# Two seams between experts, one more early tile, and layer 1's first rows turned bank by bank

## The reference

```python
def sage_conv(x, src, dst, Wl, b, Wr):          # twice per layer, relu between
    mean = segment_sum(x[src], dst) / max(count(dst), 1)
    return mean @ Wl.T + b + x @ Wr.T
x = x + gnn0(layernorm(x))
x = x + ffn0(layernorm(x))     # 8 experts, 256 -> 512 -> 256, each row takes the 2 with the best scores
x = x + gnn1(layernorm(x))
x = x + ffn1(layernorm(x))     # a shared MLP and 4 small experts, weighted top 2
# ffn0, one expert: gelu(x @ W1[e] + b1[e]) @ W2[e] + b2[e], summed over the row's two experts
```

## Time and profile before

| | us |
|---|---|
| median of 3 runs | 1255.82 (1254.37 to 1258.06) |
| profiled execution | 1258.41 |
| its span | 1256.9 |
| TensorE busy | 1170.8 (93%) |
| VectorE busy | 582.1 (46%) |
| ScalarE busy | 356.5 (28%) |
| GpSimd busy | 161.4 (13%) |

### The profile page before, as it was taken

The page is one execution under the profiler, slowest core; times in us unless marked ns, Lnnn a source line. Parts: engine busy times, 40 slices in busy tenths (PEclk is TensorE's granted clock), DMA queues, the critical chain, the costliest instruction groups (busy, mean ns, idle before and its releaser), DMA issues. The chain is left out here.

```text
span 1256.9 us, 22265 instructions
## 1 busy us (share of the span) xinstructions
PE 1170.8 (93%) x7928; PEld 884.9 (70%) x7928; DVE 582.1 (46%) x1656; ACT 356.5 (28%) x767; POOL 161.4 (13%) x152
## 2 busy tenths in 40 slices
PE   5979999998999996998999959999999999999998
PEld 3658888885667884777888746655556678876675
DVE  7978888844445768111111155100024455346644
ACT  3554444432220002322333233300012201033433
POOL 4100000000000436443344400000000000000000
PEclk9979999999999997999999969999989999998999
DMA  6500000025653336355654342110046535226101
GB/s 203 167 25 13 22 18 13 21 60 142 179 141 98 111 115 189 65 106 103 137 110 87 68 116 85 59 53 30 30 122 176 152 95 173 81 73 192 42 21 39
DMA packets 134352, 117.30 MB, mean 93 GB/s; under 512 B 23302, under 2 KB 122697, under 8 KB 134272
## 3 DMA queue, kind: packets, MB, share of 16 engines
q1 hardware_dynamic: 102640, 76.36, 21.3%
q0 software_dynamic: 12368, 18.62, 7.6%
q10 hardware_dynamic: 19264, 21.24, 4.9%
HBM read 67.01 MB, written 48.76 MB: 92 GB/s over the span
## 5 line engine op out<-in xcount | busy, mean ns | idle before, releaser
L1334 PE MATMUL b_pa<-adj,l_parts 128*128 (+2 forms) x1078 | 144.0, 285 | 3.7 <-ACT ring L1267 3.7
L1334 PEld LDWEIGHTS b_pa<-adj,l_parts 128*128 128x128 f16 x1078 | 101.0, 98 | 26.9 <-issue 5.5
L1273 ACT ACTIVATE adj<-b_pw 128x450 f32 (+1 forms) x176 | 86.6, 546 | 97.4 <-PE b_pw L1318 92.4
L2512 PE MATMUL l_sum<-l_parts,ring 128*128 128x256 f32 x448 | 104.0, 385 | 5.0 <-ACT ring L2582 2.3
L2647 POOL DMA_INDIRECT x<-ring,l_ids_now x56 | 87.5, 1562 | 132.8 <-DVE ring L2612 92.7
L601 DVE TENSOR_TENSOR ring<-it,key 128x900 f16<-128x900 f16 (+1 forms) x176 | 88.8, 547 | 30.8 <-PE b_pw L1318 30.7
L2512 PEld LDWEIGHTS l_sum<-l_parts,ring 128*128 128x128 f32 x448 | 82.9, 190 | 22.0 <-ACT ring L2582 11.9
L2612 DVE TENSOR_TENSOR ring<-l_sum,l_parts 128x256 f32 (+1 forms) x56 | 23.6, 424 | 149.1 <-PE l_sum L2512 149.1
L1318 PE MATMUL b_pw<-ring,room 128*128 128x150 f16 (+1 forms) x1056 | 78.2, 228 | 7.1 <-DVE room L601 5.3
L2176 PE MATMUL l_sum<-l_parts,adj 128*128 128x256 f16 x735 | 82.9, 273 | 1.3 <-DVE l_rows L1902 1.3
L601 DVE TENSOR_TENSOR room<-ib,low 128x1536 f16<-128x1536 f16 x88 | 83.9, 953 | 0.0
(11 more groups left out here) (398 smaller groups left out, 1704.7 us busy)
## 6 DMA issues: line engine op xcount, KB each, us to landing
ring<-sums_and_zt SPq DMA_DIRECT2D x50, 256.0 KB, 3.2
l_parts<-in_L_ffn_W SPq DMA_DIRECT2D x16, 512.0 KB, 5.5
l_parts<-slots_in SPq DMA_DIRECT2D x28, 257.0 KB, 2.9
pre<-room ACTq DMA_DIRECT2D x34, 128.0 KB, 1.7
ring<-inv SPq DMA_DIRECT2D x50, 64.0 KB, 3.6
sums_and_zt<-room ACTq DMA_DIRECT2D x5, 640.0 KB, 3.4
adj<-xt SPq DMA_DIRECT2D x5, 640.0 KB, 4.5
adj<-x SPq DMA_DIRECT2D x5, 640.0 KB, 5.6
```

What stands on the lines that cost most here:

```text
L1273: ins = nc.scalar.activation(adj[:, :, ds(group * GW * W + b * BANKW * W, BANKW * W)].rearrange("p k (w j) -> p w k j", j=W), pw[u % SLOT ...
L1334: ins = nc.tensor.matmul(pa[f][:, 0:size], parts[:, k, a, f * P:(f + 1) * P], adj[:, k, ds(r * BW, size)], start=k == 0 and a == 0, stop=k ...
L2512: ins = nc.tensor.matmul(to[t], h[:, n, t * P:(t + 1) * P], w2[:, u, n, :], start=n == 0, stop=n == HB - 1)
```

## The change

- **Seams.** `later(0)` is only the loop of steps. `later(1)` begins with a turn, the second product that expert 0 left, and the first product. Expert 2 begins with its turn and the second product that expert 1 left (`second_product_left`).
- **Early tile.** Expert 0's count is raised to at least 512 before group 4, so tile 2 (its second) has a fixed place, too; it is loaded, turned and multiplied before `tables_ready` is waited for. `CAP` grows from 3456 to 3712 slots a region and `STMAX`, the length of the tables, from 40 to 42.
- **Start.** Before the last ranking TensorE now does the turn of tile 0 and also its first product. ScalarE waits for the scatter of group 4 after its first copy instead of ahead of it. A Gelu on one column is added ahead of the stage on ScalarE. The score transposes of the last two groups go to bank 2 and no longer wait for `put` of the group before.
- **Layer 1's first rows.** The turned tiles lie two to a bank, each bank is signalled when turned and copied by one operation, and `y` of a bank waits for that bank only. The sum of squares stands behind these copies, the totals ahead of `y`'s last bank, and the scales behind VectorE's normalising of chunk 1.

```diff
-STMAX = (2 * ROWS + E0 * (2 * ST - 1)) // ST
-CAP = ROWS + ST
+EARLY_ROWS = (2 * ST,) + (ST,) * (E0 - 1)
+STMAX = -(-(2 * ROWS + sum(EARLY_ROWS) + E0 * (ST - 1)) // ST // 2) * 2
+CAP = ROWS + max(EARLY_ROWS)
...
-def transpose_chunk(nc, pe, bank, rows, ident, ready, before):
+def transpose_chunk(nc, pe, bank, rows, ident, ready, before, turned):
...
         for f in range(KD):
-            last = nc.tensor.transpose(transposed_place(bank, f, t), rows[:, t, f * P:(f + 1) * P], ident[:, :])
-    return last
+            at = (2 * f + t % 2) * P
+            last = nc.tensor.transpose(bank[t // 2][:, at:at + P], rows[:, t, f * P:(f + 1) * P], ident[:, :])
+        if t % 2 or t == CT - 1:
+            last.then_inc(turned, 1)
...
+def evacuate_transposed(nc, bank, out, n, last=False):
+    at, size = 2 * n * P, min(2, CT - 2 * n) * P
+    turned = bank[n][:, :].rearrange("p (f n) -> p f n", f=KD)[:, :, 0:size]
...
+    return nc.scalar.activation(out[:, :, at:at + size], turned, ACT.Copy)
...
         self.vector_norm(dve, 0)
-        self.vector_scales(dve)
         for c in range(1, CHUNKS):
             self.vector_norm(dve, c)
+            if c == 1:
+                self.vector_scales(dve)
             self.vector_low(dve, c - 1)
...
-        self.scalar_squares(act)
         for c in range(CHUNKS):
             self.scalar_turned(act, c)
             if c == 0:
+                self.scalar_squares(act)
                 self.scalar_norms(act)
...
-        evacuate_transposed(self.nc, self.bank, self.xt, c == CHUNKS - 1).then_inc(self.s["xt_ready"], 1)
+        for n in range(BT):
+            act.wait_ge(self.s["n_turned"], BT * c + n + 1)
+            evacuate_transposed(self.nc, self.bank, self.xt, n, c * CT + 2 * n == LAST).then_inc(self.s["xt_ready"], 1)
...
-        pe.wait_ge(s["xt_ready"], c + 1)
         for n in range(BT):
+            pe.wait_ge(s["xt_ready"], BT * c + n + 1)
+            if c == 0 and n == 0:
+                pe.wait_ge(s["weights_in"], 16 * 4)
+            if c == 0 and n == BT - 1:
+                self.tensor_totals(pe)
...
                 if c == SETTLED:
-                    rch.done(nc.vector.tensor_scalar(pre[:, 0, :], before, float(ST), None, ALU.max))
+                    rch.mark(nc.vector.tensor_scalar(pre[:, 0, 0:1], before[:, 0:1], float(EARLY_ROWS[0]), None, ALU.max))
+                    rch.done(nc.vector.tensor_scalar(pre[:, 0, 1:E], before[:, 1:E], float(ST), None, ALU.max))
...
             act.wait_ge(s["x_out"], 16 * FINISHES)
             if routing:
+                nc.scalar.activation(tmp[:, 2, 0:1], tmp[:, 2, 0:1], ACT.Gelu)
                 follow["scalar"](act)
...
+                elif routing and c >= FINISHES - 2:
+                    pe.wait_ge(s["sum_done"], STARTS[FINISHES - 1])
+                    pe.wait_ge(s["score_done"], c)
                 else:
                     pe.wait_ge(s["placed" if routing else "score_done"], c)
-                nc.tensor.transpose(last_bank[:, 0:P], flat[:, :], g["ident"][:, :]).then_inc(s["scored"], 1)
+                nc.tensor.transpose(back_bank(c)[:, 0:P], flat[:, :], g["ident"][:, :]).then_inc(s["scored"], 1)
...
                     if routing and (what, c) == ("rank", FINISHES - 1):
-                        follow["turn"]()
+                        follow["start"](pe)
...
         load(1, CAP)
+        load(2, ST)
         sp.wait_ge(table.s["tables_ready"], 1)
...
+    def start_early(pe):
+        turn_rows(pe, 0)
+        pe.wait_ge(table.s["first_w_in0"], LOADS)
+        first_products(pe, 0, 0)
...
             start, end = later_range(pe, e, tiles)
-            with pe.If(tiles > 1):
-                turn(start)
-                first_product(start, e)
+            if e == 0:
                 with pe.If(tiles > 2):
-                    with pe.Fori(pe.snap(start + 1), end) as j:
+                    with pe.Fori(start, end) as j:
                         step(j, e)
...
-                second_product(end, e)
+                return
+            with pe.If(tiles > 1):
+                turn(start)
+                second_product(start, 0)
+                first_product(start, 1)
+                with pe.If(tiles > 2):
+                    with pe.Fori(pe.snap(start + 1), end) as j:
+                        step(j, 1)
...
+        def second_product_left(at):
+            tiles = pe.value_load(g["tiles"][0:1, 0, 1:2], min_val=1, max_val=ONE_MOST)
+            with pe.If(tiles > 1):
+                second_product(at, 1)
...
             if e > 2:
                 second_product(at, 1 - u)
+            else:
+                second_product_left(at)
...
-        pe.wait_ge(table.s["first_w_in0"], LOADS)
-        first_product(0, 0)
         turn(1)
         pe.wait_ge(s["h_done"], HB)
         multiply_h(0, whole)
         pe.wait_ge(table.s["first_w_in1"], LOADS)
         first_product(1, 1)
+        turn(2)
         pe.wait_ge(s["h_done"], 2 * HB)
         multiply_h(1, whole1)
+        first_product(2, 0)
         pe.wait_ge(table.s["tables_ready"], 1)
...
-        scattered(act, [SETTLED])
-        one_tile(0, 0)
+        one_tile(0, 0, lambda: scattered(act, [SETTLED]))
         one_tile(1, 1)
+        one_tile(2, 0)
...
-            if not isinstance(j, int):
+            if not isinstance(j, int) or j >= 2:
                 dve.wait_ge(s["adding"], NT * j)
```

74 lines of the change are left out of this document (35 added, 39 removed).

## The result

| | before | after |
|---|---|---|
| median, us | 1255.09 (1253.97 to 1258.06, 4 runs) | 1245.85 (1245.14 to 1246.95, 4 runs) |
| profiled execution | 1258.41 | 1245.65 |
| its span | 1256.9 | 1244.2 |

The ratio is 0.9919, interval 0.9903 to 0.9936: 10.2 us of 1255.09, between 8.0 and 12.2 (the two medians differ by 9.2). The forecast was 11.2 off and 1244.6. By time alone the interval also holds rival B (8.6) and rival C (9.1); only the traces tell them from the forecast. The profiled executions differ by 12.8 us; before's lies 3.3 above its median, after's on it.

A forecast was written before the change was run, and what follows sets the result against it. TensorE, busy for 93% of the span, was taken as the bound, its waits in the expert stage and before layer 1 being the gain. 3.7 + 5.4 + 2.1 = 11.2 us from the median 1255.82 gave 1244.6, own range 1242.0 to 1247.5.

The forecast's parts named there:

- rival B: Expert stage start: the late ranking comes through in full, start gains only 1.1 us; 8.6 us in all, 1247.2; chance 0.13.
- rival C: Layer 1's part gives nothing, its chain running over ScalarE and the scales; 9.1 us in all, 1246.7; chance 0.14.
- The sum: Whole kernel: start 3.7, seams 5.4 and layer 1 2.1 add to a gain of 11.2 us.
- rival F: Expert stage: GpSimd's scatter-adds become the bound; 3.9 us slower, 1259.7; chance 0.04.
- Seams, forecast 5.4: Seams 0 to 1 and 1 to 2 become steady tiles of 7.74 us; gain 5.4 us.
- Start, forecast 3.7: Expert stage start: early first product, later ScalarE wait and second early tile bring second product 2 forward; gain 3.7 us.
- TensorE waiting 1.4 us, and second product 2 at 514.53: Expert stage, turn 3: TensorE waits 1.4 us for rows, then second product 2 at 514.53 instead of 518.22.
- upper bound: Expert stage start: gain of 5.1 us if turn 3's rows are there when TensorE is.
- Layer 1, forecast 2.1: Layer 1's first rows: products start 3.1 us earlier, but the chain over the scales leaves a gain of 2.1 us.
- could come earlier: Layer 1: TensorE's clock might rise sooner, giving up to 1.5 us on the products, 1 of it let through by ScalarE.
- Cost 0 for the early Gelu: ScalarE before the expert stage: the added Gelu, behind the last rows' store, costs 0, or up to 0.5 us, covered at turn 3.

The follow-up runs named there:

- scales_first: Changed kernel with VectorE's seven small operations for layer 1's scales ahead of normalising chunk 1 instead of behind it; 1251.02 us, 0.9979 of the kernel before.
- rank_inside: Changed kernel with the last group's ranking between the second and third bank of tile 0's early first product; 1243.81 us, 0.9904 of the kernel before.
- after_again: The changed kernel itself, timed again on the slower chip; 1268.35 us, 0.9907 of the kernel before on that chip.
- wait_ahead: Changed kernel with ScalarE's wait for the scatter of group 4 back ahead of its first copy; 1248.21 us, 0.9954 of the kernel before.
- no_early_gelu: Changed kernel without ScalarE's one-column Gelu that loads its table early; 1246.67 us, 0.9941 of the kernel before.
- only_start: Changed kernel with the seams put back and the old Normalise class, so the start's edits alone; slower chip, 1272.51 us, 0.9951 of the kernel before.
- only_layer1: Kernel before with only layer 1's first rows turned and copied bank by bank; slower chip, 1277.97 us, 1.0000 of the kernel before.
- filled_wait: Changed kernel with sixteen transposes into an unread bank before turn 3, where TensorE waits; 1245.91 us, 0.9919 of the kernel before.
- only_seams: Kernel before with only the two expert seams closed; slower chip, 1276.07 us, 0.9973 of the kernel before.

## Why the prediction was right, and the step that was off

**The sum** was 11.2 us; 10.2 was measured. The stage that bounds was read rightly: closed gaps of TensorE in the expert stage were gains, and no other engine came up behind it. From 495 to 712 us TensorE waited in the changed kernel only for the rows of turn 3 (2.4 us) and for the last Gelu (0.6). GpSimd's adds of the first two tiles were 7.6 us apart (510.90 to 518.48), and no second product was late for one (rival F falls).

**Seams, forecast 5.4, measured 5.3.** Every tile of the changed kernel is 7.73 to 7.75 from second product 3 to the last. The windows of seam and steady tile gave this without any view of what each wait was released by.

**Start, forecast 3.7, measured 1.8.** This is the term that was mis-sized. Reckoned from the last routing turn (484.21 and 483.69), step by step:

| | forecast | measured |
|---|---|---|
| last ranking | 12.6 | 12.2 |
| last group's first scatter | 14.5 | 14.9 |
| TensorE ready for turn 3 | 28.2 | 27.8 |
| turn 3 | 29.6 | 30.1 |
| second product 2 | 30.3 | 30.6 |
| second product 3 | 38.1 | 40.0 |

Up to second product 2 each step is within 0.6 us. The failing step is the sentence "TensorE waiting 1.4 us, and second product 2 at 514.53", which took the tile behind as a steady one. The wait was 2.36, because TensorE came 0.4 earlier and the rows 0.5 later than reckoned, and the second product behind it ran mostly at half clock: 1.6 us that stood in no term. I had priced slow clock where the trace of before showed it, behind its idle times, and not at the new idle time that I had worked out myself. How large the miss is depends on the profile: scales_first has the same start, turn 0's rows at the same time and a wait of 2.34, but no slow tile, and its S gives a gain of 3.1; so the longer wait is a miss of about 0.6, and the slow tile, in four of six profiles, most of the rest. In rank_inside, where the wait is 0.78, S is 5.1 less than before: that is the upper bound that the prediction gave for this part, and the late ranking is what kept the change from it. Rival B put the whole lateness of the ranking, 3.85, on the path; turn 3 came 1.85 later than turn 2 had before, where the forecast had 1.3. Its mechanism was there in half its size. That the start's 1.8 is nearer to B's 1.1 than to my 3.7 comes from the clock, which B did not have.

The Trainium skill (TensorE: Matmul & The Clock Gate, "HAM oscillation — how this bites in real kernels") describes a TensorE whose clock falls while it waits for transfers, so that the next products start cold. The traces agree in part: behind a wait of 2.28 to 2.58 us for rows the tile took 9.32 in four profiles (after, after_again, wait_ahead, no_early_gelu) and 7.64 in two (only_start, scales_first). And in none of the four did the products start cold: windows of 0.5 us show the granted clock at 1.00 until 0.6 to 1.3 us after the wait had ended. Why it fell in four and not in two stays open.

**Layer 1, forecast 2.1, measured 2.9.** The products started 2.18 us behind the turn's start (forecast 2.43). Normalising of chunk 1 ended 7.7 us behind the turn's start, as forecast (742.3 less 734.62). But I had the root end last, at 8.4, and it came at 6.4 to 6.6, since the clock rose between 729 and 731, during the first products, and they took 4.05 for sixteen; so the scales were done at 8.8 instead of 9.6, and these 0.8 us are most of the difference. The rise "could come earlier", as the prediction had it, but it is the smaller half of the 0.8. In rank_inside the clock rose later, and TensorE took 6.31 us from its first product to the next group, as forecast (6.23). Even so the root came at 7.7 to 7.9 and the scales were done at 9.2, and the turn of chunk 2 came only 0.33 us later than in the changed kernel, since the normalising hides the rest (L reads 30.99 all the same, as the idle time ahead of the first turn was 0.28 shorter). So the early rise is worth about 0.3, and about 0.5 is that the forecast put totals and root too late at its own pace. Rival C falls by L, with the reservation that the timing of only_layer1 leaves.

**Cost 0 for the early Gelu**: right; its load ended at 488.23, 1.06 before the copy. The reason was partly wrong: the prediction put the load behind the landing of the last rows' store, but it ran ahead of that wait, and only the Gelu waited (in filled_wait the load began at 487.29 and the Gelu, released by that transfer, at 489.39, ahead of the copy). The Trainium skill (ScalarE: Activation LUTs, "What ACT_TABLE_LOAD costs") adds a drain of 1.38 us to the load's 1.28. Where nothing else was waited for, these traces show none: the activation behind it began 0.02 us after the load's end in after (486.95 + 1.28 to 488.25), and in no_early_gelu again (496.21 + 1.28 to 497.51).

**Timing and trace.** The start and layer 1 miss in opposite directions (-1.9 and +0.8); with -0.1 of the seams that is the 1.2 by which 10.0 falls short of 11.2. That the median agrees with the forecast to 1.25 us is in part this, which is luck.

## What to carry to other kernels

Where a gap is closed upstream, work out the new idle time downstream and price the clock behind it, not only its length; between 2.3 and 2.6 us of waiting cost a further 1.7 us in four profiles of six. A wait moved behind the work that doesn't need it is worth looking for where a fixed chain (here ranking, places, scatters, rows) hangs behind that work (S 3.5 us), and here it paid only because something independent, the early tile, stood ready to be done meanwhile (S 7.6 us). Where two engines' lists meet, as at layer 1's scales, try the order on both sides on paper: here what stood blocked behind the waiting instruction cost more than what waited for it (L 3.6 us).

## What the runs showed of the hardware

- The granted clock fell, or did not, behind waits of the same length of one place: 9.32 us for the tile behind 2.28, 2.36, 2.41 and 2.58 us, and 7.64 behind 2.34 and 2.38. Where it fell, it did so 0.6 to 1.3 us after work had begun again, at a moment when TensorE was busy.
- One chip took 24 us (1.9%) longer than the others for the same kernel; its traces show short gaps in TensorE's stream ahead of the expert stage. Parts of 3 us were not measurable there with 12 runs.
- A table load on ScalarE cost its 1.28 us and nothing behind it (0.02 us to the next activation), and it ran ahead of the wait of the activation that needed it.
- Rows requested behind an expert's weights reached TensorE 4.9 us after the request once (only_seams), against 2.9 from request to landing in the median of the kernel before.
- Filling an idle time with transposes did not delay the work behind, with 16 of them for a wait of 2.4 us and with 8 for one of 0.8.
